# The copies of the attention's weighted sums, from VectorE to ScalarE and from one PSUM ring to another

## The reference, cut to what matters

```python
def _attention(x, wq, wk, wv, wo, cos, sin, causal_bias):
    ...
    scores = jnp.einsum('bhqd,bhkd->bhqk', q, k) / jnp.sqrt(jnp.asarray(HD, x.dtype))
    scores = scores + causal_bias
    attn = jax.nn.softmax(scores, axis=-1)
    out = jnp.einsum('bhqk,bhkd->bhqd', attn, v)
    out = out.transpose(0, 2, 1, 3).reshape(b, s, NH * HD)
    return out @ wo
...
for l in range(L):
    res = x
    h = _rms(x, ln1_w[l])
    h = _attention(h, wq[l], wk[l], wv[l], wo[l], cos, sin, causal_bias)
    x = jnp.clip(res + h, -100.0, 100.0)
    res = x
    h = _rms(x, ln2_w[l])
    h = _moe(h, wr[l], wg[l], wu[l], wd[l])
    x = jnp.clip(res + h, -100.0, 100.0)
```

## Time and profile before

| | us |
|---|---|
| median of 3 runs | 3139.78 (3132.79 to 3152.36) |
| the profiled execution | 3140.97 |
| its span on the core | 3136.4 |
| granted TensorE clock, mean | 0.933 of full |

### The profile page before, as it was taken

How to read it: one execution, slowest core, us unless ns; L and a number is a source line. 1 busy time by engine, 2 the same in 40 slices (tenths; PEclk the granted TensorE clock), 3 DMA queues, 4 the chain that set the end, 5 groups by cost and what they waited for, 6 DMA issues and landing times.

```text
span 3136.4 us, 66694 instructions
## 1 busy us (share of the span) xinstructions
PE 2583.6 (82%) x20342; PEld 2082.6 (66%) x20342; DVE 2343.4 (75%) x8711; ACT 1977.4 (63%) x7055; POOL 1875.0 (60%) x1701
## 2 busy tenths in 40 slices
PE   3277777999889988999889988999889978999772
PEld 2256666777677766777667766777677766777662
DVE  8887788887777777777777777777777777877553
ACT  2056666677667766767667766767667666776520
POOL 1156666556766676676766665666756666666333
PEclk9888989999999999999999999999999999999975
DMA  9512224665555535554556524453455524552584
GB/s 355 223 68 72 82 73 140 217 220 169 179 197 194 194 114 191 195 188 137 172 199 203 186 98 157 164 175 110 149 178 169 169 87 152 173 176 99 194 269 129
DMA packets 295873, 518.81 MB, mean 165 GB/s; under 512 B 40736, under 2 KB 166224, under 8 KB 295136
## 3 DMA queue, kind: packets, MB, share of 16 engines
q1 hardware_dynamic: 279136, 480.97, 45.5%
q0 software_dynamic: 16384, 33.59, 3.6%
HBM read 323.79 MB, written 106.73 MB: 137 GB/s over the span
## 4 chain that ended last, share of the span: by engine, by line
PE 49%; DVE 22%; ACT 17%; POOL 6%; issue 4%; DMA 1%; SPq 1%; POOLq 0%; DVEq 0%; ACTq 0%
ACT arena L1125 9%; PE psum L849 8%; PE psum L867 7%; PE psum L824 4%; PE psum L926 3%; PE psum L869 3%; ACT arena L1133 3%; PE psum L976 3%; PE psum L906 3%; PE psum L908 2%; PE psum L907 2%; DVE arena L1724 2%; PE psum L977 2%; PE psum L978 2%; POOL rows_in L1380 2%
## 5 line engine op out<-in xcount | busy, mean ns | idle before, releaser
L1125 ACT ACTIVATE arena<-arena 128x128 f32<-128x128 f32 (+1 forms) x2048 | 902.6, 446 | 112.4 <-DVE arena L1728 112.1
L1389 POOL TENSOR_TENSOR arena<-arena 128x512 f32<-128x512 f32 (+1 forms) x512 | 746.0, 1478 | 173.5 <-DVE arena L1733 173.5
L1404 POOL TENSOR_TENSOR arena<-arena 128x512 f32<-128x512 f32 x320 | 402.4, 1284 | 570.0 <-DMA arena<-arena 569.8
L1133 ACT COPY arena<-psum 128x384 f32<-128x384 f32 x1024 | 444.7, 482 | 273.6 <-PE psum L849 272.8
L849 PE MATMUL psum<-arena 128*128 128x128 f32 x3072 | 468.8, 291 | 179.5 <-ACT arena L1133 157.9
L849 PEld LDWEIGHTS psum<-arena 128*128 128x128 f32 x3072 | 341.8, 145 | 288.9 <-ACT arena L1133 219.6
L824 PE MATMUL psum<-arena 64*128 64x256 f32 (+1 forms) x4096 | 435.7, 346 | 54.6 <-DVE arena L1724 33.7
L1724 DVE CUSTOM_DVE_ANT_0 arena<-psum,arena 128x256 f32<-128x256 f32 x1024 | 429.2, 419 | 0.0
L1703 DVE TENSOR_TENSOR arena<-psum,arena 128x512 f32<-128x512 f32 x640 | 393.0, 678 | 3.6 <-PE psum L908 3.6
L1125 ACT ACTIVATION_READ_ACCUMULATOR arena<-arena 128x1 f32 x2048 | 389.3, 190 | 0.0
L824 PEld LDWEIGHTS psum<-arena 64*128 64x128 f32 x4096 | 312.3, 191 | 101.4 <-issue 35.2
(11 more groups left out here) (210 smaller groups left out, 5564.2 us busy)
## 6 DMA issues: line engine op xcount, KB each, us to landing
gu<-gu_kept SPq DMA_DIRECT2D x320, 512.0 KB
wd<-wd_kept SPq DMA_DIRECT2D x320, 256.0 KB
arena<-arena SPq DMA_DIRECT2D x128, 384.0 KB, 3.1
arena<-arena SPq DMA_DIRECT2D x128, 256.0 KB
arena<-rows_in SPq DMA_DIRECT2D x320, 64.0 KB
rows_out<-arena SPq DMA_DIRECT2D x320, 64.0 KB, 2.6
rows_in<-arena SPq DMA_DIRECT2D x34, 512.0 KB, 7.5
rows_out<-arena SPq DMA_DIRECT2D x34, 512.0 KB, 12.5
```

The costliest lines, as they stand in the source:

```text
L1125: ins = A.activation(a, a, ACT.Exp, bias=negmax[:, q, k:k + 1], accum_out=rowsum[:, q, k:k + 1])
L1133: A.copy(probsT[:, 4 * (q % 2) + i, :], psum[:, t_bank(key), 0:3 * P]).then_inc(sem("t_free"), 1)
L1389: ins = G.tensor_tensor(a, a, r[:, :, t:t + 1].broadcast_to([P, 4, P * (t + 1)]), ALU.mult)
L1404: G.tensor_tensor(keys_and_queries(it, u), keys_and_queries(it, u), turned_part[:, u, :], ALU.add) \
```

## The change

`copy_o` moves from VectorE to ScalarE, and its entry from ring u to ring t. In ring t each attention now has five entries. ScalarE's copy of group 2 comes after the exps of the turn's group 0, that of group 3 after the squares of the coming sequence and before the exps of group 1; those of groups 0 and 1 directly behind the copies of the slices. The number of instructions stays. The inserted lines shift those below: in the changed kernel the new copy is L1137, copy_v L1142, the copies of logits and ranks L1186 and L1191, the gate's tanh L1215.

```diff
--- before.py
+++ after.py
@@ def attend(it, q):            (number_slots)
         for i in range(4):
             t["probs", it, q, i] = len(t)
-        u["o", it, q] = len(u)
+        t["o", it, q] = len(t)
@@ TensorE
-                u_is_free(("o", it, q))
+                t_is_free(("o", it, q))
                 weigh(it, q, 0)
-                weigh(it, q, 2).then_inc(sem("u_full"), 1)
+                weigh(it, q, 2).then_inc(sem("t_full"), 1)
...
-                bank = u_bank(("o", it, q))
+                bank = t_bank(("o", it, q))
...
-                u_was_read(pe, ("o", it, 3))
+                t_was_read(pe, ("o", it, 3))
@@ ScalarE
+            def copy_o(it, q):
+                t_is_full(act, ("o", it, q))
+                A.copy(oT[:, 2 * q:2 * q + 2, :].rearrange("p a b -> p (a b)"), psum[:, t_bank(("o", it, q)), :]) \
+                    .then_inc(sem("t_free"), 1)
...
                 if now:
                     exps(it, 0)
+                if old:
+                    copy_o(it - 1, 2)
                 place(it, 1)
                 place_end(it, 1)
                 if old:
                     copy_probs(it - 1, 3)
                 if coming:
                     square_rows(it + 1)
+                if old:
+                    copy_o(it - 1, 3)
                 if now:
                     exps(it, 1)
...
                     copy_probs(it, 0)
+                    copy_o(it, 0)
...
                     copy_probs(it, 1)
+                    copy_o(it, 1)
@@ VectorE
-            def copy_o(it, q):
-                u_is_full(dve, ("o", it, q))
-                V.tensor_copy(oT[:, 2 * q:2 * q + 2, :].rearrange("p a b -> p (a b)"), psum[:, u_bank(("o", it, q)), :]) \
-                    .then_inc(sem("u_free"), 1)
...
                 place(it, 0)
-                if old:
-                    copy_o(it - 1, 2)
...
                     norm_apply(it + 2, 1)
-                if old:
-                    copy_o(it - 1, 3)
...
-                if now:
-                    copy_o(it, 0)
...
-                if now:
-                    copy_o(it, 1)
```

## The result

The change costs 1.5%: 3189.82 us (median of 4 runs, 3180.79 to 3202.93) against 3144.31 us (4 runs, 3132.79 to 3152.36), ratio 1.015 with a 95% interval of 1.0113 to 1.0186, so 46 us in the medians. The profiled execution took 3202.93 us (span 3200.5), the slowest of the four; the one of before took 3140.97. The two traces are therefore 62 us apart (64 in span), 16 us more than the change costs by the medians. A leg of a turn that is read over many turns hardly suffers from that.

The account below looks back on a forecast made before the run. Handovers bound the kernel; no engine is full. From 3140.97 us: third slice +42+5+6, ranks +10+2+2, update_x +15-2, lay-outs -17, turns 1 to 8 -17, turns 9 to 15 -6: +40, so 3180; range 3130 to 3212.

Parts of the forecast that it names:

- third slice: Before weighing, TensorE must also wait for ScalarE's third slice copy, 0.25 us each: +42 us (turns 16 to 63), +5, +6.
- ranks: ScalarE's copy of group 1's sums delays its ranks copy by 0.27 us: +10 us in turns 16 to 63, +2, +2.
- update_x: Copying group 3's sums delays group 1's exps, then update_x; scores(2) stalls 0.5 us in 30 turns: +15 us, bounds 0 and 29.
- lay-outs: In six turns behind a lay-out, group 2's weighing no longer waits for xT_lo: 2.76 us each, 17 us gained.
- early turns: Turns 1 to 8: norm statistics no longer stand behind VectorE's group 2 copy; 2.1 us each, 17 us gained, bounds 0 and 17.
- The low bound: At the third slice's wait, TensorE's existing 0.17 us idle might be saved, leaving 0.08 each: 14 us in place of 42.
- Turns 16 to 63 in sum: Third slice +42, ranks +10, update_x +15, scores(2) waits for update_x in some 14 turns -2, lay-outs -17 us.
- TensorE waits little for these copies: Of VectorE's 256 copies of the weighted sums, 175.3 us: said to cause TensorE little waiting, so removing them wins little.
- The next step, the gate matmuls, still does: In lay-out turns the gate matmuls still wait for xT_lo, so only the weighing moved into that wait is won, 2.76 us.
- The clock at group 2's weighing: Rival, 0.13: longer idle drops TensorE to 1.2 GHz there in all 35 full-clock turns, 0.9 us each: +23, 3203 us.
- Relief of VectorE: Rival, 0.10: freeing VectorE of copies is worth its full price, 57 us won against 25 of costs: 3108 us.
- The rule of the Trainium skill on banks: Independent groups should rotate through banks so copies overlap matmuls; the last weighing loses its bank outside the ring of two.

Follow-up runs that it names:

- ring-alone kernel: Against the kernel before, the weighted sums of all groups go to ring t but VectorE still copies them: 3176.84 us, ratio 1.0077.
- group 3 alone: Against the kernel before, ScalarE copies only group 3's sums, before the exps of group 1, in ring u: 3244.82 us, ratio 1.0121 (kernel before 3202.15 there).
- one head first: Against the changed kernel, ScalarE does one head of group 1's exps before copying group 3's sums: 3173.08 us, ratio 1.0081 to the kernel before.
- more at the lay-outs: Against the kernel before, around six lay-outs only: group 2's sums in ring t, ScalarE copying groups 1 (behind the ranks) and 2: 3126.79 us, ratio 0.9930.

## Why the prediction was right, and where its steps were not

The forecast was + 40 and the measured difference is + 46. The reasons given were the right ones (third slice, ranks, update_x against the lay-outs and the early turns), but that the sum came so close is in part luck: update_x was 15 us too low and the early turns' gain some 8 too high, while the lay-outs' gain was 10 too low and 9 came back behind group 2's weighing, and these nearly cancel.

**The third slice** held: 0.26 in the leg from group 0 to 1, 0.26 or 0.27 in the ring-alone kernel from 1 to 2, and 218 waits of 0.19. The low bound (the 0.17 of idle time saved) didn't come: the loads wait 0.41 where they waited 0.18. I gave 42 us to turns 16 to 63. In the leg from group 2 to 3, 0.18 of the 0.25 came back, because the gate's second product had waited for VectorE's copy of the sums in ring u (L976 for L1737, 37 times in the list above), and I had passed over this wait with "TensorE waits little for these copies". Turn 46, before and changed:

```profile
2168.40 0.50 PE L976 MATMUL psum<-gu,xT_hi 128*128 128x512 f32 x1
2168.73 0.40 PE L977 MATMUL psum<-gu,xT_hi 128*128 128x512 f32 x1
```

```profile
2203.65 0.39 PE L976 MATMUL psum<-gu,xT_hi 128*128 128x512 f32 x1
2203.88 0.40 PE L977 MATMUL psum<-gu,xT_hi 128*128 128x512 f32 x1
```

The second product followed the first by 0.87 us before (VectorE's copy ended at 2168.34, it began at 2168.40) and by 0.80 after; its own second matmul came 0.33 behind its first one before and 0.23 after. Together that is the 0.17 to 0.18. It makes 48 x 0.18 = 9 us of the 42.

**The ranks** held: 0.27 foreseen, 0.28 in the legs.

**update_x** was the step that failed in size. I had priced a stall of 0.5 in 30 turns, 15 us. The leg shows 1.0, alone (group 3 alone, 16.62) and with the rest. The prediction counted only the stop itself; the later start behind the scaled rows and the new start of the second half are the other half. The new start could have been read from the earlier trace rows (six matmuls in 0.92 us, ten in 1.14) and the earlier trace rows (sixteen in 1.63). Worth 15 us more.

**The lay-outs** were undersized: the six turns went from 295.4 to 280.8 us, though each also carries the 2.1 us that a turn now costs, so 27 us and not 17 were won there. A single trace gives this to some 8 us only: with one head first, where a turn is 0.77 shorter, the six took 284.7. VectorE, which bounds that place, lost two copies as well; the kernel with more at the lay-outs points to what they are worth, 11.4 us in the traces, some 7 by the times, with intervals that overlap. "The next step, the gate matmuls, still does" was right, and where that wait is long the granted clock behind it is lower.

**Turns 1 to 8** were oversized: 17 foreseen; turns 2 to 8 are 2.6 us longer in the trace (297.3 to 299.9), where the costs that I counted were 8. But the same instructions took 290.9 in one kernel that is as before in these turns, so a single trace can't carry this term. Timed alone it is some 8.5. My lower bound named something of GpSimd's being late in its place; half of the term went instead to VectorE's statistics, which run longer beside GpSimd.

**Turns 16 to 63 in sum**: 48 foreseen (42 + 10 + 15 - 2 - 17), 54 in the traces: by legs + 19 (0 to 1), + 42 (3 to 0), - 2 (2 to 3), - 5 (1 to 2 with the weighing of group 2). The first is 7 over 48 x 0.26, from turns at a block's end.

**Rivals.** The clock at group 2's weighing: it took over 2 us in 26 of 48 turns before and in 24 after, no difference. So 22 turns were at the full clock there and not the 35 of the prediction, and by its own count this rival would have been + 14 and not + 23. Relief of VectorE: real in lay-out turns, 27 us, not the 57 of that rival; elsewhere `combine` took back 73 of the 175 us, and VectorE's idle time went to other waits, as I had said (xT_lo's for ScalarE from 199.2 to 301.6 us). The rule of the Trainium skill on banks (Perfetto Trace Analysis, Optimizing Tensor Performance, Matmuls), which I had set against the change, gave the direction: ring t alone is 1.0077.

## What to carry to other kernels

Price a wait on a matrix engine by when its successor starts, not by the stop: what was a row of sixteen pays again for its start (0.43 us here). A copy that is moved to a less busy engine costs what it shifts on that engine's chain; find the place where the engine already waits (ahead of the ranks: 0.28 of 0.47), and don't queue work that is ready behind work that waits (one head of exps ahead: 0.77 us a turn). And look for the few turns where a relief is real: parts of the change in six turns of 64 made the kernel faster by 0.5 and 0.7%, the whole in all of them made it slower by 1.5%.

## What the runs showed of the hardware that I had not expected

VectorE's copy of the sums had kept it out of GpSimd's way: without it, the 192 instructions of `combine` took 1054 ns each and not 675, because 151 of them and not 68 ran beside GpSimd's work (0.35 us alone, 1.25 beside it). A single one of the statistics ran up to five times as long (0.43 and 2.08 us). A wait in one piece of 2.62 us ahead of 64 matmuls went with a mean granted clock of 0.75 over the 13.6 us that hold both, where with one of 0.47 it was 1.00. And in four traces ScalarE began 74 to 110 copies of group 3's slices late, by 48 to 88 us in all, with nothing on its core to hold it, in comparisons where the kernel before was 1.7% slower too.
